# First FFN of a gated transformer block: the second weight's rounding, widening and transposition, and the transposition of two groups of rows, done by other engines

## The reference

```python
def _quant_per_tensor(x):
    scale = jnp.maximum(jnp.max(jnp.abs(x)) / QMAX, EPS)
    q = jnp.clip(jnp.round(x / scale), -QMAX, QMAX).astype(jnp.int8)
    return (q, scale)
def _quant_per_channel(w):
    scale = jnp.maximum(jnp.max(jnp.abs(w), axis=1) / QMAX, EPS)
    q = jnp.clip(jnp.round(w / scale[:, None]), -QMAX, QMAX).astype(jnp.int8)
    return (q, scale)
def _dyn_quant_linear(x, w, b):
    qx, sx = _quant_per_tensor(x)
    qw, sw = _quant_per_channel(w)
    acc = jnp.matmul(qx.astype(jnp.int32), qw.T.astype(jnp.int32))
    return acc.astype(jnp.float32) * (sx * sw) + b
...
h = _dyn_quant_linear(hidden_state, w1, b1)     # w1: 2048 x 512
h = jax.nn.gelu(h, approximate=False)
return _dyn_quant_linear(h, w2, b2)             # w2: 512 x 2048
...
x = x + jnp.tanh(g_ffn[0]) * _L0_ffn_ref(_layernorm(x, axis=-1), L0_ffn_w1, ...)
```

## Time and profile before

| | |
|---|---|
| median of 3 runs | 643.41 us (643.09 to 644.05) |
| profiled execution, its span from first to last instruction | 641.4 us |
| PE busy | 611.9 us (95%) |
| DVE busy | 544.2 us (85%) |
| ACT busy | 483.0 us (75%) |
| POOL busy | 346.5 us (54%) |
| DMA issued by SP and ACT (q1) | 104.23 MB |

### The profile page before, as it was taken

How to read it: one execution, slowest core, us unless ns; L and a number is a source line. 1 busy time by engine, 2 the same in 40 slices (tenths; PEclk the granted TensorE clock), 3 DMA queues, 4 the chain that set the end, 5 groups by cost and what they waited for, 6 DMA issues and landing times.

```text
span 641.4 us, 9520 instructions
## 1 busy us (share of the span) xinstructions
PE 611.9 (95%) x2863; PEld 362.3 (56%) x2894; DVE 544.2 (85%) x1065; ACT 483.0 (75%) x725; POOL 346.5 (54%) x430
## 2 busy tenths in 40 slices
PE   5899999999999999989999999999888999999997
PEld 5677777777776445544445556555433444444443
DVE  2697888889999788986779988889898999999964
ACT  4469785766655898998672576776679999999984
POOL 2579888888874255210001111114488988898861
PEclk9999999999999999999999999999999999999999
DMA  8959896899999355128538920000115665666651
GB/s 301 377 195 305 297 317 225 266 333 341 333 296 314 135 196 197 66 61 306 219 79 177 229 91 16 16 17 1 55 44 151 189 185 174 171 180 166 181 161 51
DMA packets 127862, 118.92 MB, mean 185 GB/s; under 512 B 83456, under 2 KB 90384, under 8 KB 126672
## 3 DMA queue, kind: packets, MB, share of 16 engines
q1 hardware_dynamic: 120384, 104.23, 52.8%
q10 hardware_dynamic: 7440, 14.24, 6.5%
HBM read 68.04 MB, written 30.49 MB: 154 GB/s over the span
## 4 chain that ended last, share of the span: by engine, by line
PE 65%; DVE 13%; ACT 11%; issue 6%; DMA 2%; POOL 1%; SPq 0%; ACTq 0%; DVEq 0%; POOLq 0%
PE ps L1189 22%; PE ps L1484 14%; PE ps L1500 8%; PE ps L1309 5%; ACT turn L975 4%; PE ps L1411 3%; PE ps L1441 3%; DMA arena<-in_x 2%; ACT arena L920 2%; PE ps L1459 2%; PE ps L1415 2%; PE ps L1198 2%; PE ps L1391 1%; PE ps L1401 1%; DVE turn L1878 1%
## 5 line engine op out<-in xcount | busy, mean ns | idle before, releaser
L1189 PE MATMUL ps<-arena 128*128 128x288 f32 x640 | 160.6, 407 | 2.0 <-DVE inv_s L1671 0.8
L1189 PEld LDWEIGHTS ps<-arena 128*128 128x128 f32 x640 | 119.4, 190 | 34.1 <-issue 1.0
L1484 PE MATMUL ps<-arena 128*128 128x512 bf16 x510 | 113.4, 379 | 4.1 <-DVE arena L2073 4.0
L1484 PEld LDWEIGHTS ps<-arena 128*128 128x128 bf16 x512 | 49.6, 98 | 65.9 <-issue 4.1
L687 POOL TENSOR_TENSOR arena<-arena 128x512 f32<-128x512 f32 x64 | 80.3, 1275 | 8.9 <-DVE arena L2073 8.0
L585 POOL TENSOR_TENSOR arena<-arena 128x1024 f32<-128x1024 f32 x32 | 60.6, 1893 | 16.7 <-issue 11.5
L1500 PE MATMUL ps<-arena 128*128 128x512 bf16 x241 | 57.1, 379 | 1.9 <-ACT arena L1089 0.7
L1309 PE MATMUL ps<-arena 128*128 128x512 bf16 (+1 forms) x248 | 56.2, 379 | 0.9 <-ACT arena L920 0.4
L1353 PE MATMUL ps<-arena 128*128 128x512 bf16 x250 | 55.3, 379 | 0.7 <-DVE arena L1822 0.4
L592 POOL TENSOR_TENSOR turn<-turn 128x512 f32<-128x512 f32 x31 | 40.5, 1305 | 23.5 <-DVE turn L1648 23.5
L2073 DVE SCALAR_TENSOR_TENSOR arena<-ps,up_scale,arena 128x512 f32<-128x512 f32 x64 | 46.7, 745 | 5.8 <-ACT arena L1065 5.0
(11 more groups left out here) (233 smaller groups left out, 1296.1 us busy)
## 6 DMA issues: line engine op xcount, KB each, us to landing
arena<-in_L_ffn_w SPq DMA_DIRECT2D x48, 512.0 KB, 6.3
arena<-kpad_d ACTq DMA_DIRECT2D x16, 512.0 KB, 7.1
hq_d<-arena SPq DMA_DIRECT2D x14, 512.0 KB, 2.7
tern_d<-late SPq DMA_DIRECT2D x24, 256.0 KB, 5.6
arena<-in_ctx SPq DMA_DIRECT2D x4, 1024.0 KB, 12.1
arena<-in_x SPq DMA_DIRECT2D x4, 1024.0 KB, 14.8
arena<-in_L_ffn_w ACTq DMA_DIRECT2D x8, 512.0 KB, 6.0
arena<-in_ctx SPq DMA_DIRECT2D x2, 2048.0 KB, 10.4
```

Of the source, the lines that this page charges most:

```text
L1189: last = pe.matmul(ps[:, 4 * s + lo, 0:NB * PAIRS], toep[:, u, (LB - 1 - lo + li) * P:(LB - lo + li) * P], kv[:, s, li, :], start=(li == 0 ...
L1484: last = pe.matmul(ps[:, bank, :], xq4T[:, s, 4 * j + k, :], w[:, k, c * L:(c + 1) * L], start=(k == 0), stop=(k == LB - 1))
```

## The change

Block c of the second weight: POOL rounds it itself (`w2_quant` in POOL's program) into one of two slots of `w2i`; SP stores it to DRAM (`w2q_d`) and reads it back with a transposing DMA into `fw2T`; POOL widens it there in place (`w2_widen`). Groups 2 and 3 of the quantised rows: SP stores `wqi` to `x1q_d` and reads it back with a transposing DMA into `xqT`, where DVE widens it in place (`turned_widen`). PE's 32 + 64 transposes, ACT's four `w2_quant` and its copy of block 3, and DVE's copies out of PSUM for both are gone. ACT waits for all four row scales (`w2_scaled`) before `diag`. PE waits for `w2_ready` where it waited for `w2T_out`.

```diff
-            for g in range(NG):
+            def x1_save(g):
                 t = order1[G * g]
                 sp.wait_ge(S["xb_added"], G * g + G)
                 rows = slice(t, t + TB * (G - 1) + 1, TB)
                 sp.dma_start(x1_d[:, rows, :], x_res[:, rows, :]).then_inc(S["x1_saved"], 16)
-            for c in range(2, LB):
-                sp.wait_ge(S["w2_used"], c - 1)
-                if c == LB - 1:
-                    sp.wait_ge(S["xqb_ready"], NG + 1)
-                sp.dma_start(raw2[c], w2c[c]).then_inc(w2_in[c % 2], 16)
-            sp.wait_ge(S["w2T_made"], LB)
+
+            def x1_turned(g):
+                sp.wait_ge(S["xqi_ready"], g + 1)
+                sp.dma_start(x1q_d[g - 2].rearrange("(n p) k -> p n k", p=P),
+                             wqi[:, g % 2, :].rearrange("p (n k) -> p n k", n=G)).then_inc(w1_out[g - 2], 16)
+                sp.wait_ge(w1_out[g - 2], 16 * W1_STORES + 16)
+                sp.dma_start_transpose(xqT[:, :, g * L:(g + 1) * L].bitcast(I16), x1q_d[g - 2]).then_inc(w1_raw[g - 2], 16)
+
+            def w2_store(c):
+                sp.wait_ge(S["w2_used"], c + 1)
+                sp.dma_start(w2q_d[c * P:(c + 1) * P, :], w2i[:, c % 2, :]).then_inc(tint_out[c], 16)
+                if c + 2 < LB:
+                    sp.dma_start(raw2[c + 2], w2c[c + 2]).then_inc(w2_in[c % 2], 16)
+
+            def w2_turned(c):
+                sp.wait_ge(tint_out[c], 16 * TERN_STORES + 16)
+                sp.dma_start_transpose(w2_block(c).bitcast(I16), w2q_d[c * P:(c + 1) * P, :]).then_inc(traw_in[c], 16)
...
-            pool.wait_ge(S["xqb_ready"], NG + 1)
+            pool.wait_ge(S["xqi_ready"], NG)
             for t in order1[10:]:
                 pool.tensor_tensor(x_res[:, t, :], x_res[:, t, :], b2b[:, :], ALU.add).then_inc(S["xb_added"], 1)
-            pool.wait_ge(S["xq_tr"], NG + 1)
-            for c in range(LB):
-                pool.wait_ge(S["w2_used"], c + 1)
-                if c >= 1:
-                    pool.wait_ge(S["w2T_made"], c)
-                pool.tensor_scalar(w2b, w2i, 1.0, 0.0, ALU.mult, ALU.add).then_inc(S["w2b_ready"], 1)
+
+            def w2_quant(c):
+                pool.wait_ge(S["w2_scaled"], c + 1)
+                if c >= 2:
+                    pool.wait_ge(tint_out[c - 2], 16 * TERN_STORES + 16)
+                pool.tensor_scalar(w2i[:, c % 2, :], raw2[c], iw2[:, c:c + 1], None, ALU.mult).then_inc(S["w2_used"], 1)
...
-            gelu(1, 3, range(12))
-            act.wait_ge(S["xq_tr"], NG + 1)
-            w2_quant(0)
-            gelu(1, 3, range(12, FT))
+            gelu(1, 3, range(FT))
             act.wait_ge(S["x1_saved"], 16 * NG)
...
-            act.wait_ge(S["w2T_made"], LB)
-            act.activation(*w2T_place(LB - 1), ACT.Copy).then_inc(S["w2T_out"], 1)
             act.wait_ge(S["swb_made"], 1)
...
-            mm1(1, range(FT // 2))
-            rows_T(2)
-            rows_T(3)
-            mm1(1, range(FT // 2, FT))
+            mm1(1, range(FT))
 
             pe.wait_ge(S["xq_out"], NG)
             with pe.Fori(0, 2) as r:
-                mm1(r + 2, range(4))
-                w2_T(2 * r, 0)
-                mm1(r + 2, range(4, 12))
-                w2_T(2 * r + 1, 1)
-                mm1(r + 2, range(12, FT))
+                mm1(r + 2, range(FT))
...
-            pe.wait_ge(S["w2T_out"], LB + 2)
+            pe.wait_ge(S["w2_ready"], LB)
```

More of the change, by code:

```diff
@@ L338, in up_banks, with w2_block @@
             return ((3, 5), (4, 6), (0, 1), (3, 5))[c]
-        def w2T_place(c):
-            return fw2T[:, :, c * P:(c + 1) * P], bank_bf(4 + 2 * (c % 2), 2).rearrange("p (f o) -> p f o", f=FT)
+        TERN_LOADS, TERN_STORES, W1_LOADS, W1_STORES = 2 * TC // 4, TC // 4, WC // 4, WC // 2
+        def w2_block(c):
+            return fw2T[:, :, c * P:(c + 1) * P]
         @block.sync
@@ L434, in _ @@
                 sp.dma_start(x1_d[:, rows, :], x_res[:, rows, :]).then_inc(S["x1_saved"], 16)
-            for c in range(2, LB):
-                sp.wait_ge(S["w2_used"], c - 1)
-                if c == LB - 1:
-                    sp.wait_ge(S["xqb_ready"], NG + 1)
-                sp.dma_start(raw2[c], w2c[c]).then_inc(w2_in[c % 2], 16)
-            sp.wait_ge(S["w2T_made"], LB)
+            def x1_turned(g):
[12 more added lines that the diff above has]
+                sp.dma_start_transpose(w2_block(c).bitcast(I16), w2q_d[c * P:(c + 1) * P, :]).then_inc(traw_in[c], 16)
+            x1_save(0)
+            x1_turned(2)
+            x1_save(1)
+            x1_turned(3)
+            x1_save(2)
+            x1_save(3)
+            w2_store(0)
+            w2_store(1)
+            w2_turned(0)
+            w2_turned(1)
+            w2_store(2)
+            w2_turned(2)
+            w2_store(3)
+            w2_turned(3)
             for j, w in ((1, phi_w_d), (2, g_w_d)):
@@ L630, in _, with w2_widen @@
                 pool.tensor_tensor(x_res[:, t, :], x_res[:, t, :], b2b[:, :], ALU.add).then_inc(S["xb_added"], 1)
-            pool.wait_ge(S["xqb_ready"], NG + 1)
+            pool.wait_ge(S["xqi_ready"], NG)
             for t in order1[10:]:
                 pool.tensor_tensor(x_res[:, t, :], x_res[:, t, :], b2b[:, :], ALU.add).then_inc(S["xb_added"], 1)
-            pool.wait_ge(S["xq_tr"], NG + 1)
-            for c in range(LB):
-                pool.wait_ge(S["w2_used"], c + 1)
-                if c >= 1:
-                    pool.wait_ge(S["w2T_made"], c)
-                pool.tensor_scalar(w2b, w2i, 1.0, 0.0, ALU.mult, ALU.add).then_inc(S["w2b_ready"], 1)
+            def w2_quant(c):
[3 more added lines that the diff above has]
+                pool.tensor_scalar(w2i[:, c % 2, :], raw2[c], iw2[:, c:c + 1], None, ALU.mult).then_inc(S["w2_used"], 1)
+            def w2_widen(c):
+                pool.wait_ge(traw_in[c], 16 * TERN_LOADS + 16)
+                pool.tensor_scalar(w2_block(c), w2_block(c).bitcast(I16), 1.0, 0.0, ALU.mult, ALU.add).then_inc(S["w2_ready"], 1)
+            pool.wait_ge(S["xq_tr"], 3)
+            w2_quant(0)
+            w2_quant(1)
+            w2_widen(0)
+            w2_widen(1)
+            w2_quant(2)
+            w2_quant(3)
+            w2_widen(2)
+            w2_widen(3)
             pool.wait_ge(S["hmax_ready"], 1)
@@ L937, in _ @@
             quant_x(3)
[L939 to L943, removed]
-            gelu(1, 3, range(12))
-            act.wait_ge(S["xq_tr"], NG + 1)
-            w2_quant(0)
-            gelu(1, 3, range(12, FT))
-            act.wait_ge(S["x1_saved"], 16 * NG)
[L950 to L954, removed]
+            gelu(1, 3, range(FT))
+            act.wait_ge(S["x1_saved"], 16 * NG)
+            gelu(2, 0, range(FT))
             gelu(3, 1, range(4))
-            w2_quant(3)
+            act.wait_ge(S["w2_scaled"], LB)
             act.wait_ge(S["k_stored"], 16 + 16 * NB)
@@ L1147, in _ @@
             pe.wait_ge(S["consts_set"], 10)
[L1150 to L1155, removed]
             def q_tiles(g):
@@ L1755, in rows_widen, with turned_widen @@
                 v.wait_ge(S["xqi_ready"], g + 1)
-                if g >= 2:
-                    v.wait_ge(S["xq_tr"], g)
                 v.tensor_copy(wqb[:, g % 2, :], wqi[:, g % 2, :]).then_inc(S["xqb_ready"], 1)
+            def turned_widen(g):
+                rows = xqT[:, :, g * L:(g + 1) * L]
+                v.wait_ge(w1_raw[g - 2], 16 * W1_LOADS + 16)
+                v.tensor_copy(rows, rows.bitcast(I16)).then_inc(S["xq_out"], 1)
             hid_all = hid.rearrange("p q f n -> p (q f n)")
@@ L1791, in _ @@
             v.tensor_tensor(ath[:, :], ath[:, :], smean[:, :], ALU.mult).then_inc(S["btot_ready"], 1)
[L1793 to L1800, removed]
+            turned_widen(2)
             for n in range(4):
                 hid_max(n + 4, 4 * L * n + 3 * FT * L)
+                if n == 0:
+                    turned_widen(3)
+                if n >= 2:
+                    w2_scales(n)
             for n in range(7):
                 hid_max(n + 8, 4 * L * n)
[L1805 to L1808, removed]
-                    w2_out(2)
             for f in range(G):
```

18 lines of the change are left out of this document (4 added, 14 removed).

## The result

The changed kernel takes 656.39 us (median of 4 runs, 655.8 to 657.04) against 643.38 us of the kernel before on the same chip (643.09 to 644.05): ratio 1.0199, interval 1.0185 to 1.0214. It is 13.0 us slower; the prediction had 643.5 and a range up to 646.5. The profiled execution spans 654.7 us, 13.3 more than before; PE is busy 610.6 us (611.9 before), ACT 477.2 (483.0), DVE 544.6 (544.2), POOL 369.9 (346.5), and q1 moves 110.52 MB (104.23). The 96 transposes of PE and the four roundings and the copy of ACT are gone, as the change promised. PE's busy time falls by 1.3 us alone, since the matmuls of the two products take 2.5 us more in all (57.1 and 56.9 us against 56.2 and 55.3), part of them at a lower clock. POOL has 23 us more, where the prediction's own terms for it were 8.

The account below looks back on a forecast made before the run. Bound: the combination of the maxima, behind the second weight on POOL (286.2 against 286.44). -0.25 - 0.3 + 0.65 = +0.1 us on 641.4 gives 641.5, with 2.0 around it 643.5; own range 642.2 to 644.7, outer limits 640.9 and 646.5.

Parts of the forecast that it names:

- Strand 1: PE and ACT up to the first product's last tile: ready at 278.5, its gelu at 279.3, a ceiling of 6.0 us.
- Strand 2: DVE's row scales and maxima, waiting for the loads of blocks 2 and 3: last maximum at 284.8.
- loads 2 and 3: Loads of weight blocks 2 and 3, behind POOL's roundings: in at 258.9 and 263, DVE waiting from about 254.
- Strand 3: Second weight through POOL, SP and DMA: 2.0 us a rounding, last widening at 286.2, only then the combination of the maxima.
- The queue of DMAs: Transfers ahead of and within the second weight's way: 2.85 us per MB, 2.6 us per transposing transfer.
- The first rival: Queue quicker than priced, DVE decides: combination at 284.0, time 641.2, or 640.7 without the slow PE start; chance 0.30.
- PE's slow start: PE idles 6 us before the second product, then slow matmuls lose 1.5 us; 0.65 reaches the path, bounds 0 and 1.5.
- The second one: Second weight becomes the bound at POOL's wait for transposition 3: combination at 289.0, time 646.3; chance 0.28.
- the first pair of DMAs: Transposing DMAs of weight blocks 0 and 1, slowed by other traffic: 1.5 us more in the slower case.
- The closing list: What would prove it wrong: POOL's rounding much over 2.8 us, transpositions overtaking loads, or PE stalling beyond 5 us at 251.

Follow-up runs that it names:

- two_widen: round_two with the widenings of weight blocks 2 and 3 moved from POOL to DVE; 644.0 us, ratio 1.0008 to the kernel before.
- round_act: The changed kernel with the second weight's four roundings back on ACT between the gelus; 647.99 us, ratio 1.0070 to the kernel before.
- round_two: The changed kernel with POOL's roundings written as two operations (times scale, plus 0.0) instead of one; 651.57 us, ratio 1.0119 to the kernel before.
- micro: A small program without the block, copying x to the output and timing POOL operations, some with a DVE operation beside them; one run, 114.71 us.
- warm: two_widen with 112 instead of 22 unused matmuls between the two products; 642.75 us, ratio 0.9989 to the kernel before.
- early2: Kernel before with second weight by DMAs, two-operation POOL roundings, blocks 0 and 1 rounded earlier, both last x saves before the first transposition; 640.15 us, ratio 0.9950.

## Why the prediction was wrong

*Strand 1 (PE and ACT).* The work that left them did leave; I had the last tile at 278.5 and it came at about 283.5. In two_widen, where no one-operation rounding holds DVE and PE does not stop at 254, it came at 279.2; so most of the 5 us is that stop and the slow clock after it (0.69 and 0.50 in the windows from 254 to 258). Here it cost nothing, since POOL was later by far. In round_act, without the stop, the last maximum came only 0.5 us earlier.

*Strand 2 (DVE).* Last maximum done at 284.8 predicted, 285.7 measured (285.57 + 0.17). The waits for loads 2 and 3 were 1.10 and 1.07 us, where the prediction had DVE idle from about 254 to 259: the held widening moved the two maxima before load 2 to 257.9, and DVE had nothing to lose by it. In round_two the first wait is 5.86 us, as forecast.

*Strand 3, the rounding: the first failed step.* "I take 2.0", between 1.9 and 2.8; it took 5.44. Shape and number of values were matched; the form was not. The earlier trace rows are both operations with two arithmetic steps (L639 multiplies and adds 0.0; L675 multiplies by -1 and adds a column, where the prediction read a scale per row), the new one has `None` for the second. No tensor_scalar of the kernel before on POOL has that form, and my bounds came from one that only looks alike. The Trainium skill ("GPSIMD Engine Reference", 4.1 Engine selection) calls POOL roughly line-rate for one input; the 1.90 us for two operations fit that, beside DVE's 2.28 us for a maximum over as many values in the earlier trace rows; micro's 5.37 us for one operation do not. Its price, by round_two against the changed kernel, is 656.39 - 651.57 = 4.8 us.

*Strand 3, behind its end: the second failed step.* "POOL widens, 1.95: 286.2. Only then can POOL combine the maxima." It can only do so some 6 us after its last ordinary instruction: 5.79 to 6.71 us in micro and in five kernels. In the earlier trace rows the combination has 9.76 us of idle time before it that is put down to DVE, and the pause lay unseen inside. The prediction put the start of the combination at nothing; an idle time that is put down to a wait can hide a fixed cost, and a change that fills the idle time brings it out. By two_widen against round_two, 7.6 us hang on what stands on POOL ahead of the combination (651.57 - 644.0): the pause of 6.2 us, and the rest the last widening, done at 287.5 where the last maximum was there at 285.7. The two failed steps together are 12.4 of the 13.0 us; the 0.6 us left are two_widen against the kernel before, which its runs do not tell from nothing.

*The queue of DMAs* was priced well: in round_two, where the roundings have their forecast length, ten steps of strand 3 end 1.3 us late (287.5 against 286.2). The first rival (a quicker queue) is out, and no run shows that the DMAs made the kernel slow.

*PE's slow start* was expected at 1.5 us and measured at 1.55. The prediction let 0.65 of its 1.5 us arrive on the path; in two_widen the slow start is 1.87 us and warm gives 1.25 us of time for it, so about two thirds arrive there. The printed clock, 1.00 in the earlier trace rows, is 0.50 here: that doubt is settled, and the Trainium skill's rule of an idle TensorE that falls to the lower clock ("TensorE: Matmul & The Clock Gate", Part 1) agrees.

*The rivals.* The second one (the weight becomes the bound, slower) names the right place and sign, at 646.3 instead of 656.4, and with the wrong carriers: of the 1.5 us that it laid on the first pair of DMAs at most 0.7 came (block 1 is widened at 270.65 in round_two, forecast 269.9), the rounding took 5.44 where that rival had 2.8, and the pause was in no rival. My chance for slower was 0.28. The closing list named "POOL's rounding much over 2.8 us" as what would make it wrong.

## What to carry to other kernels

Before a price is taken from a row, compare the whole form of the instruction with the new one, the number of arithmetic operations too, and if the form stands in no row, let the bound be wide. An idle time ahead of an instruction that waits is only an upper limit of slack: a fixed start cost can hide in it, so leave such an instruction alone behind an engine that was idle (early2) or move the work ahead of it elsewhere (two_widen). Offloading pays when the work starts early enough to be ready well before its wait, and when nothing urgent stands behind it on an in-order queue; the second weight's way through DRAM goes with +13.0 us as it was changed here and with -3.0 us in early2.

## What was not expected of the hardware

- POOL's tensor_scalar on 128x2048 with one arithmetic operation takes 5.37 to 5.44 us, with two 1.90 (int16 to bf16) or 1.98 us (f32 to int16). With 256 values it is about 0.9 us.
- POOL pauses 5.8 to 6.7 us between an ordinary instruction and PARTITION_ALL_REDUCE and, in the one case that micro has, 7.0 us on the way back, with none between two all-reduces. The Trainium skill ("GPSIMD Engine Reference", 1.1 Terminology) tells of kernel libraries that a DMA loads into POOL's instruction memory while it runs. If that is the pause, the runs don't show it: micro has not one DMA packet between 83 and 89 us. What POOL does in it stays open.
- A DVE widening can be held until POOL's instruction has ended (5.57 and 5.83 us for 0.69); a DVE maximum beside one is not (2.29). The Trainium skill ("SBUF — State Buffer", "SBUF: two separate sides") has this as a lock between POOL and certain forms of DVE instruction, which whoever starts first holds for the whole instruction; micro agrees that one blocks the other for a whole instruction, and either can be the one that waits (DVE 5.83 for 0.69, or POOL 5.98 for 5.44); starts 0.06 to 0.08 us apart don't tell who came first.
- A transposing DMA issued behind 1 MB transfers held SP for 8.06 us, and two in round_two for 11.13, against 2.06 in the earlier trace rows.
